# Two gated feed forward layers in split fp32: a low rank bank accumulated onto a negated copy, one VectorE sum less per group, and another queue order at the start

## The chip, the cores and the metric

The program runs on one core of a Trainium2 chip. The metric is device time in microseconds. Each execution is one launch of the whole computation. TensorE (PE) multiplies matrices, VectorE (DVE), ScalarE (ACT) and GpSimd (POOL) work on elements, SyncE (SP) only starts transfers. Each engine takes its own instructions in the order of the program, and engines wait for one another through semaphores.

## What is computed

1024 tokens of width 512 (8 blocks of 128) go through two gated feed forward layers, the first with a low rank addition chosen per block, the second behind an RMS norm, and the input is added at the end:

```python
def lora_add(base, inp, A, B):
    Ab = A[layer_idx][lora_indices]
    Bb = B[layer_idx][lora_indices]
    t = jnp.einsum('bri,bni->bnr', Ab, inp)
    return base + jnp.einsum('bor,bnr->bno', Bb, t) * SCALE
gate = lora_add(jnp.einsum('bnh,fh->bnf', x, W_gate), x, A_gate, B_gate)
up = lora_add(jnp.einsum('bnh,fh->bnf', x, W_up), x, A_up, B_up)
act = jax.nn.silu(gate) * up
down = lora_add(jnp.einsum('bnf,hf->bnh', act, W_down), act, A_down, B_down)
...
nx = x * jax.lax.rsqrt(var + RMS_EPS) * ln_w
g = jnp.einsum('bsh,ih->bsi', nx, gate_w)
u = jnp.einsum('bsh,ih->bsi', nx, up_w)
return jnp.einsum('bsi,hi->bsh', jax.nn.silu(g) * u, down_w)
...
x = x + _L0_ffn_ref(_L0_cond_ref(x, ...), ...)
```

The first layer has 1376 hidden features (ten tiles of 128 and a short one of 96), the second 1792 (14 tiles).

## The kernel before

**Precision.** Every fp32 operand is held as a high part (a rounding copy, made by ScalarE, names `hi_...`) and a low part (the difference, made by VectorE, names `lo_...`). A product of two 128x128 blocks with 512 tokens is three matmuls: high by high, high by low, low by high (`PASSES`).

**Fewer products.** The layers use a seven product scheme (Strassen's, in the form with shared sums) on 2x2 blocks: two feature tiles by two halves of the tokens (t = 0 and 1). A **group** j is one such 2x2 problem for gate or up; groups 0 to 7 (`S1` = 8) belong to the first layer, even j to gate and odd j to up. Its seven products on TensorE are `q1`, `g_prod`, `p6`, `q2`, `p3`, `p7`, and `p4`, each six matmuls. `p4(j-1)` is issued in group j, between `g_prod(j)` and `p6(j)`. In groups 0 to 7 `group_loras(j)` adds the low rank part between `p3` and `p7`: two matmuls of 256 columns each for `A_BANK`, `G_BANK` and `L_BANK` (which is `bank7`), and two more at the end of `p4`. The stacked low rank weights (`stack`) come in five chunks, copied by ScalarE (`stack_hi`) and completed by VectorE (`stack_lo`).

**Sums of products** go through copies between PSUM banks and the tile `mu`: ScalarE makes `ca(j)` (q1 into `B_BANK`), `cm(j)` (g into `mu`) and `cu(j)` (p6's bank into `mu`), and silus `c11`, `c12`, `c21`, `c22`; VectorE adds and multiplies (`c12`, `c22_sum`, `c22_act`, `c11`, `c21`). TensorE waits for `ca(j)` before `p6(j)`, for `cm(j)` before `p3(j)`, for `cu(j)` before `p7(j)` and for the first sum of `c22_sum(j-1)` (semaphore `s_b22`) before `p4(j-1)`. The second sum of `c22_sum(j)` subtracts the first from `L_BANK` and frees that bank for the next group's loras (`s_l22r`).

**Weights of group j + 1** are prepared during group j: `sums` (three sums on VectorE), `hi_a` and `hi_b` on ScalarE (blocks and sums), `lo_a` and `lo_b` on VectorE. The number in `lo_a(3)` is that of the load; load 2 belongs to group 0, load 3 to group 1. q1 needs the blocks (`lo_a`), `g_prod` the sums (`lo_b`).

**The start.** Before group 0 TensorE computes two feature tiles (units 0 to 3) and the short tile without the scheme. `short(t)` also projects the tokens on the low rank A; VectorE multiplies this by a mask (`t_mask`, out `traw`), ScalarE makes its high parts twice (`t_hi`, out `tgu`), VectorE its low part (`t_lo`), and then `first_loras(t)` can run. The scheme's four token sums are made by VectorE (`x_sum(0, i)`, out `xsum_c`), split by ScalarE (`hi_x`, out `xs`) and VectorE (`lo_t`); they are T1 to T4. T4 is first needed by `p4(0)`. ScalarE splits it in `last_block`. `short(1)` needs `unit_mul(0)` on VectorE before its second eighth.

**After group 7** the down projection begins with `main_c(0, 0)`. TensorE waits for the split down weights (`hi_wd`, `lo_wd`, out `wdc`), for the split activations (`hi_ac`, `lo_ac`, out `xs`), and for all `c11` of the first layer:

```python
pe.wait_ge(s_adlo, B)
pe.wait_ge(s_c11[0], S1 // 2)
pe.wait_ge(s_c11[1], S1 // 2)
...
    pe.wait_ge(s_alo, n + 1)
    pe.wait_ge(s_wdlo, n + 1)
```

VectorE's `group(7)` issues `lo_wd(0)` and `lo_ac(0)` ahead of `c11(7)` and `c12(7)`. All orders are written out by hand in the queue of each engine.

Of the kernel before, what the change touches and what calls it, by code (L numbers as in the profile page):

```python
# [22 lines left out]
S1, S2 = G1 - 2, G1 + NF - 4  # L23
# [20 lines left out]
def build(nc, xT_in, idx_in, wsh_in, w0_in, wgu_in, wd_in, vs_in, vj_in, agu_in, bgu_in, ad_in, bd_in, lnw_in, out):  # L44
# [4 lines left out]
    with ctx:  # L49
# [185 lines left out]
        s_s12, s_s22 = sem("c12_silu"), sem("c22_silu")  # L235
        s_c12, s_b22, s_l22r = sem("c12_summed"), sem("c22_summed"), sem("c22_with_lora")
        s_c12f, s_c22f = sem("c12_act"), sem("c22_act")
# [158 lines left out]
        def _(a):  # L396
# [37 lines left out]
            def cm(j):  # L434
                a.wait_ge(s_g, j + 1)
                if j >= 2 and j % 2 == 0:
                    a.wait_ge(s_b22, j - 1)
                elif j >= 2:
                    a.wait_ge(s_c22f, j // 2)
                copy(mu[:, j % 2, 0, :], G_BANK[j % 2][:, :]).then_inc(s_cm, 1)  # L440

# [24 lines left out]
            def c22(j):  # L466
                part = act_at(tiles_of(j)[1], 1)
                if j < S1:
                    a.wait_ge(s_l22r, j + 1)
                else:  # L470
                    a.wait_ge(s_b22, j + 1)
                silu(part, part, 1.0 if j < S1 else -1.0).then_inc(s_s22, 1)
# [208 lines left out]
            hi_a(2)  # L681
            a.wait_ge(s_xsum[0], 2)
            hi_x(0, T_SLOT[1], xsum_c[:, 1])
# [4 lines left out]
            t_hi(0)  # L688
            a.wait_ge(s_raw0_ld[1], 16 * 4)
            stack_rows(0, 1, slice(0, 32))  # L690
            unit_silu(0)
            unit_silu(1)
            short_silu(0)
            stack_rows(0, 1, slice(64, KS))
            stack_hi(1, 0)
# [133 lines left out]
        def _(v):  # L829
# [39 lines left out]
            def c22_sum(j):  # L869
                v.wait_ge(s_p7, j + 1)  # L870
                v.wait_ge(s_cm, j + 1)
                part, m5 = act_at(tiles_of(j)[1], 1), mu[:, j % 2, 0, :]
                to = part if j % 2 == 0 else m5
                nc.vector.tensor_tensor(to, m5, B_BANK[j % 2][:, :], ALU.add).then_inc(s_b22, 1)
                if j < S1:
                    v.wait_ge(s_b22, j + 1)
                    v.wait_ge(s_l22, j + 1)
                    nc.vector.tensor_tensor(to, L_BANK[:, :], to, ALU.subtract).then_inc(s_l22r, 1)

            def c22_act(j):  # L880
                part, m5 = act_at(tiles_of(j)[1], 1), mu[:, j % 2, 0, :]
                v.wait_ge(s_s22, j // 2 + 1)
                if j < S1:
                    v.wait_ge(s_l22r, j + 1)
                else:
                    v.wait_ge(s_b22, j + 1)
                nc.vector.scalar_tensor_tensor(part, m5, 1.0 if j < S1 else -1.0, part, ALU.mult, ALU.mult
# [426 lines left out]
        def _(pe):  # L1314
# [426 lines left out]
```

## Time and profile before

| what | value |
|---|---|
| median of three runs | 411.17 us (410.97 to 411.42) |
| profiled execution, its own time | 411.44 us |
| its span, first to last instruction | 409.4 us |
| TensorE busy | 401.3 us, 98% |
| VectorE busy | 319.7 us, 78% |
| ScalarE busy | 235.9 us, 58% |
| granted TensorE clock | 1.000 |

In the profile, PE is a matmul and PEld a weight load; busy matmul times are modelled to their ends, and neighbours overlap. A line such as L398 or L831 is that of a helper (`copy`, `sub`), so the tiles tell which step it is.

### The profile page before, as it was taken

What the parts mean: (1) busy time and instruction counts of PE and PEld (TensorE: products, weight loads), DVE (VectorE), ACT (ScalarE), POOL (GpSimd) and SP (SyncE); (2) the same over time, 40 slices, a digit from 0 to 9 for tenths busy, and PEclk for the clock granted to TensorE, in tenths of its full rate; (3) what the DMA queues carried; (4) which work ended last, traced back from release to release, by engine and by line L of the source; (5) the groups of instructions that cost most, each with busy time, mean ns of one, the idle gap of its engine ahead of it and who ended that gap; (6) DMA issues with size and microseconds to landing.
All of it is one profiled execution on the core that took longest, in us unless ns stands there. A gap on an engine that the chain in (4) does not pass through costs nothing.

```text
span 409.4 us, 5438 instructions
## 1 busy us (share of the span) xinstructions
PE 401.3 (98%) x1849; PEld 334.2 (82%) x1849; DVE 319.7 (78%) x491; ACT 235.9 (58%) x369; POOL 12.8 (3%) x16
## 2 busy tenths in 40 slices
PE   8989999999999999999999999999999999999996
PEld 6879788888888888888888888888888888888884
DVE  4699979696957567463889988779787869899992
ACT  4789785757563467631656555555655375384640
POOL 6300000000000100000000000000000000000000
PEclk9999999999999999999999999999999999999999
DMA  7630233311111420300101113132221125105112
GB/s 255 196 115 2 78 109 112 109 51 53 51 53 52 129 78 0 104 0 0 53 0 50 54 51 103 53 102 58 98 98 58 51 90 171 75 0 194 51 51 104
DMA packets 14237, 31.87 MB, mean 78 GB/s; under 512 B 2306, under 2 KB 4610, under 8 KB 14210
## 3 DMA queue, kind: packets, MB, share of 16 engines
q1 hardware_dynamic: 13632, 29.96, 23.2%
q10 hardware_dynamic: 578, 1.57, 1.1%
q8 instruction: 14, 0.23, 0.2%
q14 instruction: 13, 0.11, 0.1%
HBM read 29.43 MB, written 2.10 MB: 77 GB/s over the span
## 4 chain that ended last, share of the span: by engine, by line
PE 92%; DVE 4%; DMA 1%; issue 1%; ACT 1%; DVEq 0%; SPq 0%
PE bank L1320 45%; PE bank L1645 16%; PE bank L1510 15%; PE bank L1428 5%; PE bank L1456 3%; PE bank L1523 2%; PE bank L1330 2%; PE bank L1475 1%; PE bank L1464 1%; DMA wraw<-w_in 1%; DVE stack L831 1%; DVE xsum_c L1089 1%; ACT tgu L398 1%; PE bank L1530 0%; DVE act L916 0%
## 5 line engine op out<-in xcount | busy, mean ns | idle before, releaser
L1320 PE MATMUL bank<-xs,ws 128*128 128x512 f32 x840 | 194.2, 390 | 1.0 <-ACT mu L398 1.0
L1320 PEld LDWEIGHTS bank<-xs,ws 128*128 128x128 f32 x840 | 156.6, 188 | 33.2 <-ACT mu L398 1.4
L1510 PE MATMUL bank<-xs,wdc 128*128 128x512 f32 x264 | 62.9, 389 | 0.0
L1510 PEld LDWEIGHTS bank<-xs,wdc 128*128 128x128 f32 x264 | 49.3, 188 | 10.1
L398 ACT ACTIVATE xs<-act 128x512 fp32r<-128x512 f32 x71 | 43.0, 624 | 21.1 <-DVE act L981 7.5
L831 DVE TENSOR_TENSOR xs<-act,xs 128x512 fp32r<-128x512 f32 x71 | 47.6, 685 | 4.7 <-ACT xs L398 4.2
L831 DVE TENSOR_TENSOR ws<-wraw,ws 128x256 fp32r<-128x256 f32 (+2 forms) x49 | 32.4, 670 | 13.6 <-ACT ws L398 13.6
L398 ACT ACTIVATE bank<-bank 128x512 f32<-128x512 f32 x22 | 12.7, 580 | 45.7 <-PE bank L1320 45.7
L1645 PE MATMUL bank<-xs,vs 128*128 128x512 f32 x168 | 38.2, 389 | 0.0
L1645 PEld LDWEIGHTS bank<-xs,vs 128*128 128x128 f32 x168 | 31.5, 188 | 6.5
L398 ACT ACTIVATE ws<-wraw 128x256 fp32r<-128x256 f32 (+2 forms) x47 | 28.6, 620 | 11.7 <-PE bank L1320 4.1
L831 DVE TENSOR_TENSOR ws<-wsum,ws 128x1024 fp32r<-128x1024 f32 x20 | 24.5, 1226 | 12.7 <-ACT ws L398 12.7
L398 ACT ACTIVATE mu<-bank 128x512 f32<-128x512 f32 x40 | 23.9, 597 | 13.6 <-PE bank L1320 12.9
L1645 PE MATMUL bank<-xs,ws 128*128 128x512 f32 x126 | 29.0, 389 | 0.0
L1645 PEld LDWEIGHTS bank<-xs,ws 128*128 128x128 f32 x126 | 23.7, 188 | 4.9
L398 ACT ACTIVATE stack<-bgu_raw 32x1024 fp32r<-32x1024 f32 (+1 forms) x20 | 22.8, 1138 | 0.3
L1428 PE MATMUL bank<-xs,ws 128*128 128x512 f32 x96 | 22.1, 389 | 0.0
L451 ACT ACTIVATE act<-bank 128x512 f32<-128x512 f32 (+1 forms) x30 | 17.4, 593 | 7.6 <-PE bank L1330 6.2
L398 ACT ACTIVATE ws<-wsum 128x1024 fp32r<-128x1024 f32 x20 | 21.1, 1053 | 0.0
L1428 PEld LDWEIGHTS bank<-xs,ws 128*128 128x128 f32 x96 | 18.0, 188 | 3.7
L831 DVE TENSOR_TENSOR wdc<-wdr,wdc 128x512 fp32r<-128x512 f32 x11 | 7.6, 690 | 11.9 <-ACT wdc L398 11.8
L398 ACT ACTIVATE wdc<-wdr 128x512 fp32r<-128x512 f32 x11 | 6.9, 629 | 15.0 <-DMA wdr<-wd_in 15.0
(124 smaller groups left out, 446.1 us busy)
## 6 DMA issues: line engine op xcount, KB each, us to landing
wraw<-wgu_in SPq DMA_DIRECT2D x22, 512.0 KB, 3.4
wdr<-vs_in SPq DMA_DIRECT2D x7, 512.0 KB, 3.4
wdr<-wd_in SPq DMA_DIRECT2D x11, 256.0 KB, 2.7
wraw<-vj_in SPq DMA_DIRECT2D x3, 896.0 KB, 4.6
xa<-xT_in SPq DMA_DIRECT2D x4, 256.0 KB, 4.7
wraw<-w_in SPq DMA_DIRECT2D x4, 256.0 KB, 4.9
xa<-xT_in ACTq DMA_DIRECT2D x2, 512.0 KB, 6.4
bgu_raw<-bgu_in SPq DMA_DIRECT2D x32, 32.0 KB, 1.7
```

Source lines behind the costliest of these rows:

```text
L398: return nc.scalar.activation(out_ap, in_ap, ACT.Copy, scale=scale)
L451: return nc.scalar.activation(out_ap, in_ap, ACT.Silu, scale=scale)
L831: return nc.vector.tensor_tensor(out_ap, raw, v32(part), ALU.subtract)
L1089: nc.vector.scalar_tensor_tensor(s[:, i], s[:, min(i - 1, 1)], -1.0, half, ALU.mult, ALU.subtract).then_inc(s_xsum[ph], 1)
L1320: ins = mm(z[:, :], ws[:, j % 2, w, s, k * P:(k + 1) * P], xs[:, c, r, k, :], start=(start and k == 0 and s == 0 and r == 0), stop=(k == 1 ...
L1330: ins = mm(z[0:m, half], stk[c % 2][:, 2 * t + q, cols], t_op[:, half], start=(alone and q == 0), stop=(q == 1), skip_group_check=True)
L1428: ins = mm(z[:, :], ws[:, j % 2, w, s, (k % 2) * P:(k % 2) * P + P], x_op(k, t, r), start=(k == 0 and s == 0 and r == 0), stop=(k == KT - ...
L1456: mm(UNIT_BANK[i][g][:, :], w0_tile(s, k, g, i), x_op(k, 0, r), start=(k == 0 and s == 0 and r == 0), stop=(k == KT - 1 and r == 1), skip_ ...
L1464: mm(UNIT_BANK[n][g][:, :], w0_tile(s, k, g, UNITS[n][0]), x_op(k, 1, r), start=(k == 0 and s == 0 and r == 0), stop=(k == KT - 1 and s == ...
L1510: ins = mm(z[:, :], wd[:, s, h * P:(h + 1) * P], x[r], start=(start and s == 0 and r == 0), stop=False, skip_group_check=True)
L1523: ins = mm(T_BANK[t][:, :], ad[:, n, t, :], slot_c(u, r), start=(first and r == 0), stop=(last and r == 1), skip_group_check=True)
L1645: ins = mm(DOWN[p][3][h][:, :], down_w(i, s)[:, h * P:(h + 1) * P], slot_f(i, r), start=(p < 2 and k == 0 and s == 0 and r == 0), stop=(k ...
```

## The change

In groups 0 to 7 `cm(j)` now copies -G from its bank into `L_BANK`. The L loras accumulate onto it, a new ScalarE copy `cl(j)` takes the result to `mu` at the end of the group, and `c22_sum(j)` is one subtraction of `B_BANK`. TensorE no longer waits for `s_l22r` ahead of the L loras. At the start `t_mask(0)` and `t_hi(0)` come before the second token sum and its copy, the last four small low rank A splits come after `t_lo(0)` on VectorE, the second stack chunk's copies come after the silus, and `x_sum(0, 3)`, its copy and its low part come later.

```diff
             def cm(j):
                 a.wait_ge(s_g, j + 1)
+                if j == 0:
+                    a.wait_ge(s_um, 3)
+                elif j < S1:
+                    a.wait_ge(s_cl, j)
+                else:
+                    mu_free(j)
+                if j < S1:
+                    copy(L_BANK[:, :], G_BANK[j % 2][:, :], -1.0).then_inc(s_cm, 1)
+                else:
+                    copy(mu[:, j % 2, 0, :], G_BANK[j % 2][:, :]).then_inc(s_cm, 1)
...
+            def cl(j):
+                a.wait_ge(s_l22, j + 1)
+                mu_free(j)
+                copy(mu[:, j % 2, 0, :], L_BANK[:, :]).then_inc(s_cl, 1)
...
             def group(j, last):
                 ca(j)
-                if j == 0:
-                    last_block()
...
                 cu(j)
+                if j == 0:
+                    last_block()
                 if j + 1 < last:
                     hi_b(w_of(j + 1))
...
                 if j % 2 == 0:
                     c11(j)
+                if j < S1:
+                    cl(j)
...
-                nc.vector.tensor_tensor(to, m5, B_BANK[j % 2][:, :], ALU.add).then_inc(s_b22, 1)
                 if j < S1:
-                    v.wait_ge(s_b22, j + 1)
-                    v.wait_ge(s_l22, j + 1)
-                    nc.vector.tensor_tensor(to, L_BANK[:, :], to, ALU.subtract).then_inc(s_l22r, 1)
+                    v.wait_ge(s_cl, j + 1)
+                    nc.vector.tensor_tensor(to, m5, B_BANK[j % 2][:, :], ALU.subtract).then_inc(s_b22, 1)
...
             stack_lo(0, 0)
-            x_sum(0, 1)
             v.wait_ge(s_maskr, 1)
             t_mask(0)
+            x_sum(0, 1)
+            lo_t(0, 0)
+            t_lo(0)
             for b in range(4, B):
                 lo_agu(b)
-            lo_t(0, 0)
-            t_lo(0)
...
                     lo_a(w_of(j + 1))
+                    if j == 0:
+                        x_sum(0, 3)
                     lo_b(w_of(j + 1))
+                if j == 0:
+                    lo_t(0, 3)
...
-                if j >= 1:
-                    pe.wait_ge(s_l22r, j)
-                else:
+                if j == 0:
                     pe.wait_ge(s_tneg, 1)
-                    pe.wait_ge(s_um, 3)
-                group_lora(L_BANK, j, 1, 1, alone=True).then_inc(s_l22, 1)
+                group_lora(L_BANK, j, 1, 1).then_inc(s_l22, 1)
```

VectorE's queue at the first mask, before (the row of `traw` is `t_mask(0)`, that of `tgu` is `t_lo(0)`, `short_w_lo` are the small splits):

```order
L1089 SCALAR_TENSOR_TENSOR xsum_c<-xsum_c,xa1 128x1024 [waits x_sum_c]
L922 TENSOR_TENSOR traw<-bank0,mask 32x512 [waits short_projected,mask_repeated]
L922 TENSOR_TENSOR traw<-bank5,mask 32x512
L831 TENSOR_TENSOR short_w_lo<-agu_raw,xs 128x2x4x16 [waits agu_hi] x4
L831 TENSOR_TENSOR xs<-xsum_c,xs 128x1024 [waits x_hi_c]
L831 TENSOR_TENSOR tgu<-traw,tgu 32x1024 [waits t_masked,t_hi]
```

and now:

```order
L934 TENSOR_TENSOR traw<-bank0,mask 32x512 [waits short_projected,mask_repeated]
L934 TENSOR_TENSOR traw<-bank5,mask 32x512
L1101 SCALAR_TENSOR_TENSOR xsum_c<-xsum_c,xa1 128x1024 [waits x_sum_c]
L846 TENSOR_TENSOR xs<-xsum_c,xs 128x1024 [waits x_hi_c]
L846 TENSOR_TENSOR tgu<-traw,tgu 32x1024 [waits t_masked,t_hi]
L846 TENSOR_TENSOR short_w_lo<-agu_raw,xs 128x2x4x16 [waits agu_hi] x4
```

The token sum moved behind the mask products, and the small splits behind `t_lo(0)`.

ScalarE's queue in group 0, before (`ca(0)`, `last_block`, `cm(0)`, `hi_a(3)`, `cu(0)`, `hi_b(3)`, `c11(0)`):

```order
L398 ACTIVATE bank2<-bank0 128x512 [waits unit_silu,q1_done]
L398 ACTIVATE xs<-xsum_c 128x1024 [waits unit_up,x_sum_c]
L398 ACTIVATE mu<-bank5 128x512 [waits g_done]
L398 ACTIVATE ws<-wraw 128x3x256 [waits unit_up,w_loaded_odd]
L398 ACTIVATE mu<-bank2 128x512 [waits p6_done]
L398 ACTIVATE ws<-wsum 128x4x256 [waits w_sums,unit_up,w_loaded_odd]
```

and now, up to `cl(0)`:

```order
L398 ACTIVATE bank2<-bank0 128x512 [waits unit_silu,q1_done]
L398 ACTIVATE bank7<-bank5 128x512 [waits unit_act,g_done]
L398 ACTIVATE ws<-wraw 128x3x256 [waits unit_up,w_loaded_odd]
L398 ACTIVATE mu<-bank2 128x512 [waits p6_done]
L398 ACTIVATE xs<-xsum_c 128x1024 [waits unit_up,x_sum_c]
L398 ACTIVATE ws<-wsum 128x4x256 [waits w_sums,unit_up,w_loaded_odd]
L467 ACTIVATE act<-bank0 128x512 [waits q2_done]
L398 ACTIVATE mu<-bank7 128x512 [waits l22_done]
```

The copy of the token sum moved from ahead of `cm(0)` to between `cu(0)` and `hi_b(3)`, and the copy out of `bank7` is new.

ScalarE's queue at the end of group 7, before (`c21(6)`, `cu(7)`, then `hi_wd(0)`, `hi_ac(0)`, `hi_wd(1)`):

```order
L451 ACTIVATE act<-bank2 128x512 [waits p4_done]
L398 ACTIVATE mu<-bank4 128x512 [waits c12_act,p6_done]
L398 ACTIVATE wdc<-wdr 128x512 [waits stack_lo,wd_loaded_even]
L398 ACTIVATE xs<-act 128x512 [waits g_done,unit_act]
L398 ACTIVATE wdc<-wdr 128x512 [waits wd_loaded_odd]
```

and now:

```order
L467 ACTIVATE act<-bank2 128x512 [waits p4_done]
L398 ACTIVATE mu<-bank4 128x512 [waits c12_act,p6_done]
L398 ACTIVATE mu<-bank7 128x512 [waits c22_act,l22_done]
L398 ACTIVATE wdc<-wdr 128x512 [waits stack_lo,wd_loaded_even]
L398 ACTIVATE xs<-act 128x512 [waits g_done,unit_act]
L398 ACTIVATE wdc<-wdr 128x512 [waits wd_loaded_odd]
```

Here `cl(7)`, with its wait for the L loras, came in ahead of `hi_wd(0)`.

## Rows read from the trace of the kernel before

**Rows 1.** The page, busy us, share of the span and instructions of each engine

```profile
PE 401.3 (98%) x1849; PEld 334.2 (82%) x1849; DVE 319.7 (78%) x491; ACT 235.9 (58%) x369; POOL 12.8 (3%) x16
```

**Rows 2.** Busy time by stretch: from:to, its length, busy by engine, PEclk, DMA share, GB/s

```profile
27.00:52.00 25.00, 22.70 (x133) 19.63 (x133) 23.90 (x28) 20.62 (x25) 0.00 (x0) 1.00 0.12 35
30.83:47.60 16.77, 16.77 (x106) 15.16 (x105) 16.36 (x19) 14.05 (x16) 0.00 (x0) 1.00 0.17 48
50.45:405.70 355.25, 355.19 (x1600) 294.73 (x1600) 278.68 (x432) 199.55 (x321) 2.79 (x4) 1.00 0.22 70
```

**Rows 3.** Instructions in time order, the first mask: start, us, engine, line, operation, [idle before]

```profile
23.14 1.22 DVE L1089 SCALAR_TENSOR_TENSOR xsum_c<-xsum_c,xa 128x1024 f32<-128x1024 f32 x1
...
24.40 1.30 DVE L922 TENSOR_TENSOR traw<-bank,mask 32x512 f32<-32x512 f32 x2
...
25.36 0.89 ACT L398 ACTIVATE xs<-agu_raw 128x128 fp32r<-128x128 f32 x4
...
25.73 0.90 DVE L831 TENSOR_TENSOR short_w_lo<-agu_raw,xs 128x128 fp32r<-128x128 f32 x4
26.16 2.13 ACT L398 ACTIVATE tgu<-traw 32x1024 fp32r<-32x1024 f32 x2
26.55 1.22 DVE L831 TENSOR_TENSOR xs<-xsum_c,xs 128x1024 fp32r<-128x1024 f32 x1
...
27.51 0.84 PE L1464 MATMUL bank<-xs,first_w 128*128 128x512 f32 x3
...
28.32 1.22 DVE L831 TENSOR_TENSOR tgu<-traw,tgu 32x1024 fp32r<-32x1024 f32 x1 [0.56 <-ACT tgu L398]
...
29.64 1.67 PE L1330 MATMUL bank<-tgu,stack 128*128 128x256 f32 x12 [1.29 <-issue]
...
30.83 1.28 DVE L916 TENSOR_TENSOR act<-act,bank 128x512 f32<-128x512 f32 x2
...
31.15 0.64 PE L1475 MATMUL bank<-xs 128*128 128x256 f32 x4
```

**Rows 4.** Instructions in order of time, groups 0 and 1

```profile
42.38 1.59 PE L1330 MATMUL bank<-tgu,stack 128*128 128x256 f32 x12
...
43.81 5.63 PE L1320 MATMUL bank<-xs,ws 128*128 128x512 f32 x24
...
47.60 1.22 DVE L1089 SCALAR_TENSOR_TENSOR xsum_c<-xsum_c,xa 128x1024 f32<-128x1024 f32 x1
...
48.86 1.06 ACT L398 ACTIVATE xs<-xsum_c 128x1024 fp32r<-128x1024 f32 x1 [2.88 <-DVE xsum_c L1089]
...
50.45 1.65 PE L1320 MATMUL bank<-xs,ws 128*128 128x512 f32 x6 [1.01 <-ACT mu L398]
...
52.61 1.23 DVE L831 TENSOR_TENSOR ws<-wsum,ws 128x1024 fp32r<-128x1024 f32 x1 [0.26 <-ACT ws L398]
52.66 5.63 PE L1320 MATMUL bank<-xs,ws 128*128 128x512 f32 x24
...
54.35 0.68 DVE L874 TENSOR_TENSOR act<-mu,bank 128x512 f32<-128x512 f32 x1
...
58.12 0.40 PE L1330 MATMUL bank<-tneg,stack 128*128 128x256 f32 x2
```

**Rows 5.** Instructions in order of time, the end of group 7

```profile
123.06 0.60 ACT L398 ACTIVATE mu<-bank 128x512 f32<-128x512 f32 x1 [0.79 <-PE bank L1320]
123.56 0.62 ACT L398 ACTIVATE wdc<-wdr 128x512 fp32r<-128x512 f32 x1
...
125.58 0.88 PE L1330 MATMUL bank<-tgu,stack 128*128 128x256 f32 x6
126.02 0.69 DVE L894 TENSOR_TENSOR act<-act,bank 128x512 f32<-128x512 f32 x1 [0.51 <-PE bank L1330]
...
127.68 2.88 PE L1510 MATMUL bank<-xs,wdc 128*128 128x512 f32 x12
```

**Rows 6.** Instructions in order of time, TensorE's warm-up

```profile
1.14 3.86 PE L1439 MATMUL bank<-ones 128*128 128x512 f32 x9 [1.14 <-DVE eps L1097]
```

More of the change, by code:

```diff
@@ L235, in build @@
         s_s12, s_s22 = sem("c12_silu"), sem("c22_silu")
-        s_c12, s_b22, s_l22r = sem("c12_summed"), sem("c22_summed"), sem("c22_with_lora")
+        s_c12, s_b22, s_cl = sem("c12_summed"), sem("c22_summed"), sem("l22_copied")
         s_c12f, s_c22f = sem("c12_act"), sem("c22_act")
@@ L435, in cm, with mu_free @@
                 a.wait_ge(s_g, j + 1)
+                if j == 0:
[8 more added lines that the diff above has]
+                    copy(mu[:, j % 2, 0, :], G_BANK[j % 2][:, :]).then_inc(s_cm, 1)
+            def mu_free(j):
                 if j >= 2 and j % 2 == 0:
@@ L439, in cm @@
                     a.wait_ge(s_c22f, j // 2)
-                copy(mu[:, j % 2, 0, :], G_BANK[j % 2][:, :]).then_inc(s_cm, 1)
+            def cl(j):
+                a.wait_ge(s_l22, j + 1)
+                mu_free(j)
+                copy(mu[:, j % 2, 0, :], L_BANK[:, :]).then_inc(s_cl, 1)
             def cu(j):
@@ L467, in c22 @@
                 part = act_at(tiles_of(j)[1], 1)
-                if j < S1:
-                    a.wait_ge(s_l22r, j + 1)
-                else:
-                    a.wait_ge(s_b22, j + 1)
+                a.wait_ge(s_b22, j + 1)
                 silu(part, part, 1.0 if j < S1 else -1.0).then_inc(s_s22, 1)
@@ L681, in _ @@
             hi_a(2)
-            a.wait_ge(s_xsum[0], 2)
-            hi_x(0, T_SLOT[1], xsum_c[:, 1])
+            t_hi(0)
             a.wait_ge(s_short, 1)
@@ L687, in _ @@
                 hi_agu(b)
-            t_hi(0)
-            a.wait_ge(s_raw0_ld[1], 16 * 4)
-            stack_rows(0, 1, slice(0, 32))
+            a.wait_ge(s_xsum[0], 2)
+            hi_x(0, T_SLOT[1], xsum_c[:, 1])
             unit_silu(0)
@@ L693, in _ @@
             short_silu(0)
+            a.wait_ge(s_raw0_ld[1], 16 * 4)
+            stack_rows(0, 1, slice(0, 32))
             stack_rows(0, 1, slice(64, KS))
@@ L870, in c22_sum @@
                 v.wait_ge(s_p7, j + 1)
-                v.wait_ge(s_cm, j + 1)
                 part, m5 = act_at(tiles_of(j)[1], 1), mu[:, j % 2, 0, :]
                 to = part if j % 2 == 0 else m5
-                nc.vector.tensor_tensor(to, m5, B_BANK[j % 2][:, :], ALU.add).then_inc(s_b22, 1)
                 if j < S1:
-                    v.wait_ge(s_b22, j + 1)
-                    v.wait_ge(s_l22, j + 1)
-                    nc.vector.tensor_tensor(to, L_BANK[:, :], to, ALU.subtract).then_inc(s_l22r, 1)
+                    v.wait_ge(s_cl, j + 1)
+                    nc.vector.tensor_tensor(to, m5, B_BANK[j % 2][:, :], ALU.subtract).then_inc(s_b22, 1)
+                else:
+                    v.wait_ge(s_cm, j + 1)
+                    nc.vector.tensor_tensor(to, m5, B_BANK[j % 2][:, :], ALU.add).then_inc(s_b22, 1)
             def c22_act(j):
@@ L882, in c22_act @@
                 v.wait_ge(s_s22, j // 2 + 1)
[L883 to L886, printed above, removed]
+                v.wait_ge(s_b22, j + 1)
                 nc.vector.scalar_tensor_tensor(part, m5, 1.0 if j < S1 else -1.0, part, ALU.mult, ALU.mult
@@ L1152, in _ @@
             stack_lo(1, 1)
-            x_sum(0, 3)
             def group(j, first, last):
@@ L1163, in group @@
                     sums(w_of(j + 1))
-                if j == 0:
-                    lo_t(0, 3)
                 if j > S1 and j % 2 == 0:
@@ L1393, in group_loras @@
                 group_lora(G_BANK[j % 2], j, 0, 1).then_inc(s_p3, 1)
-                if j >= 1:
-                    pe.wait_ge(s_l22r, j)
-                else:
+                if j == 0:
                     pe.wait_ge(s_tneg, 1)
-                    pe.wait_ge(s_um, 3)
-                group_lora(L_BANK, j, 1, 1, alone=True).then_inc(s_l22, 1)
+                group_lora(L_BANK, j, 1, 1).then_inc(s_l22, 1)
             def p7(j):
@@ L1550, in _ @@
                     p4(S1 - 1)
-                    pe.wait_ge(s_l22r, S1)
+                    pe.wait_ge(s_b22, S1)
                     t_c(0, 0, True, False).then_inc(s_use, 1)
```

## The prediction, made before the changed kernel ran

> **What bounds the kernel now.** I read the busy shares first, then busy time by stretch, then the rows in order of time around the places the change touches. TensorE is busy 98% of the span and VectorE 78% [rows 1], so an operation taken from VectorE is worth something only where TensorE waits for VectorE. From 50.45 to 405.70 us TensorE is busy 355.19 of 355.25 us; between 27 and 52 us it is busy 22.70 of 25 [rows 2]. So the group loop has no pause that could be won. There are two pauses worth looking at, both before it.
>
> Pause A: the first low rank products start at 29.64 after 1.29 us idle, and 0.10 before that VectorE ended its `tgu` low part, 28.32 + 1.22 = 29.54 [rows 3]. Undisturbed they would start at 27.51 + 0.84 - 0.16 = 28.19, since in an unbroken stream a group starts 0.16 before the modelled end of the one ahead (42.38 + 1.59 against 43.81 [rows 4]). A costs 1.45.
>
> Pause B: p3(0) starts at 50.45 after 1.01 idle and waited for ScalarE's `mu` copy, which stood behind the copy of the fourth token sum, started at 48.86 when VectorE ended that sum (47.60 + 1.22) [rows 4]. Undisturbed it would start at 43.81 + 5.63 - 0.16 = 49.28. B costs 1.17. Together 2.62 us can be won at most.
>
> **Mask first (A).** VectorE is free at 23.14, where the second token sum starts [rows 3]. Now the two mask products (1.30) come first and end at 24.44, and ScalarE makes both high parts from 24.48 to 26.61 (2.13 [rows 3]). VectorE: sum 24.47 to 25.69, low part of T1 25.61 to 26.83 (neighbours on all 128 rows overlap by 0.08, as 25.73 + 0.90 against 26.55), then the `tgu` low part 26.86 to 28.08. With the release of 0.10 that is 28.18 against 28.19: A is gone.
> Behind it stands what was put off. Four small low parts (0.90) run 28.11 to 29.01, the low part of T2 (1.22) 28.93 to 30.15; its high part is ready near 28.5 (26.61, the four small copies of 0.89, one copy of 1.06). So unit_mul(0) runs 30.07 to 30.75 (0.76 earlier than now, 30.83 [rows 3]), and TensorE sees it about 30.83. It needs it at the second 0.72 us piece of short(1): before, 31.15 + 0.72 = 31.87, a margin; now 28.19 + 1.51 + 0.72 = 30.42. (0.72 is (42.38 - 31.15 - 5.46) / 8, with 5.46 for 24 matmuls from 52.66 to 58.12 [rows 3, 4].) A new pause of 0.4; TensorE is 1.04 ahead after it, 1.0 with the slower first step after a pause (p3(0), below).
>
> **Fourth sum later (B).** ScalarE's copy of g(0) no longer stands behind it, and TensorE at p3(0) doesn't wait. But the sum now stands ahead of two other things that group 1 needs. On VectorE it comes after the three weight sums and lo_a(3), and ScalarE waits for it in `last_block` ahead of hi_b(3); lo_b(3) then waits for hi_b(3). VectorE did not stop between 30.83 and 47.60 (16.36 busy of 16.77 [rows 2], the rest is hand-over), so it enters this part 0.75 early. The same work that now ends where lo_b(3) starts, 52.61, less its idle 0.26 and less the low part of T4 (1.14 with overlap), then ends at 52.61 - 0.26 - 1.14 - 0.75 = 50.46 [rows 4]. From there: copy 1.06 and hi_b, another 1.06 on as many elements, 0.1 overlapped, to 52.5; lo_b(3), 1.23, ends at 53.8. TensorE needs it for g(1) at 52.66 + 2 x 1.365 - 1.0 - 1.3 = 53.1: a pause of 0.75. Then low part of T4, c12(0) and c22_sum(0) follow. That last one ends at 54.35 + 0.68 now [rows 4]; less 0.75, less 0.26, and with the new idle time of 2.1 it ends at 56.1. TensorE needs it for p4(0), which starts now at 58.12 - 1.365 = 56.76, and would start at 56.2. The first product after a pause takes 0.13 longer: p3(0) took 1.49 to the next start, not 1.365 (52.66 less 0.72 for the loras less 50.45 [rows 4]). **Gain left when p4(0) has run: 56.76 - 56.2 - 0.13 = 0.4 us of the 2.6.** The bounds: 0 if VectorE's chain slips by 0.4, 2.6 if ScalarE's wait is hidden. I take 0.4: both ends of that chain are read from rows of the same form.
>
> **Low rank bank on the negated copy.** VectorE loses eight sums of about 0.7 (as the row at 54.35 [rows 4]); TensorE's instructions are the same, and it loses its wait for VectorE ahead of the L products. ScalarE gains eight copies out of `bank7`, 0.60 each (the `mu` copy at 123.06 [rows 5]); the copy of G goes to the bank in place of `mu` at the same size. In groups 0 to 6 the new copy starts 0.92 after the first lora (six steps of 0.12, from twelve in 43.81 - 42.38 [rows 4], then 0.2 for the last to end and release) and falls in time in which ScalarE is free. Two stack copies of the size of the copy at 48.86 (1.06 [rows 4]) follow it, to 0.92 + 0.5 + 2.1 = 3.5 after the loras start. q1 of the next group, whose copy is ScalarE's next work, ends at 0.72 + 1.365 x 2 + 0.2 = 3.65, and TensorE needs that copy only for p6, some 3 us on. Covered, price zero; the end of the saved sums too, since TensorE doesn't wait there.
>
> **Group 7 is where it isn't covered.** There the next thing in ScalarE's queue is the first high part of the down weights. It now starts at 123.56, straight behind cu(7), and its like for the activations follows; c11(7) on VectorE waits only for the loras and starts at 126.02. TensorE takes main_c(0, 0) at 127.68 without a pause [rows 5]. In the new queue cl(7) stands ahead of both copies and waits for the last lora of group 7: 125.58 + 0.92 = 126.50. Then `wdc` high part 127.00 to 127.63, activation high part to 128.14; VectorE's `wdc` low part 127.66 to 128.34, activation low part 128.26 to 128.95, and c11(7), behind them in VectorE's queue, 128.87 to 129.56. main_c(0, 0) waits for both low parts and for c11(7): it starts at 129.63, not 127.68. With 0.13 for the first step that is **a new pause of 2.1 us**, in the time of the kernel before. Bounds: 1.4 if TensorE needed only the two low parts, 2.2 with 0.1 more of release. I take 2.1, the queue order fixes it. What follows (c22_sum(7), p4(7), the next weights, whose load waits for the low parts) moves with it, and TensorE runs unbroken to the end, so nothing is given back.
>
> **Sum.** -0.4 + 2.1 = +1.7 us. The profiled execution took 411.44 (span 409.4), 0.27 over the median 411.17. I forecast 413.1 for a profiled run and 411.17 + 1.65 = 412.8 for the median, 0.4% slower.
>
> **Rivals.**
> 1. Full recovery at the start, the pause in group 7 stays: -2.6 + 2.1 gives 410.6 to 410.7, no change that can be told. For it: A and B each have one named waiter. Against it: the margins above of -0.4 and -0.75 us.
> 2. Faster: the copies of group 7 are done before TensorE needs them, and 0.4 to 2.6 remains, 408.6 to 410.8. From the start of cl(7) to TensorE's release are 3.13 us, so it decides if that copy starts before 127.68 - 3.13 = 124.55. The last lora starts at 126.2 [rows 5], which speaks against it.
> 3. The new copy delays each group: it pushes the small `ad` copies of group 6 by 0.5, and by my count TensorE's p4(6) keeps 0.3. If such margins fail in two or three groups by 0.3, the time is 413.5 to 414.
> 4. The clock falls in the new pause. The granted clock stays 1.00 through pauses of 1.29 and 1.01 [rows 2, 3, 4], but this one is 1.95. The nine warm-up matmuls at 1.14 took 3.86, so 0.43 each [rows 6] against 0.228 later (5.46 / 24): half speed for 3.86 us costs 1.9 more, 414.7. The Trainium skill (TensorE: Matmul & The Clock Gate, HAM oscillation) says that idle gaps between bursts of matmuls send the engine back to 1.2 GHz; by that rule this case, by the two rows at full clock after a pause my forecast. No run here shows a pause this long.
>
> **How the numbers follow.** A measurement of this kernel can tell about 0.2%, 0.8 us, from no change. Forecast 0.73, rival 1 0.12, rival 2 0.06, rival 3 0.05, rival 4 0.04. The range takes the forecast with start gains of 0 to 1.2 and an end price of 1.9 to 2.2 (411.7 to 413.5) and reaches down to rival 1: 410.6 to 413.6. The forecast itself falls within 0.2% in some 3 of 73. Faster 0.07, same 0.15, slower 0.78.
>
> **What would show it.** Right: no idle before the first loras and before p3(0); small pauses at the second piece of short(1), g(1) and p4(0); one of about 2 us before the first `wdc` matmul, with ScalarE's copy out of `bank7` straight ahead of its first `wdc` copy. Wrong: TensorE unbroken there, or more than 1.5 us won before group 2, or idle time inside groups 2 to 7.

## The result and the profile after

The changed kernel takes 413.26 us (median of 13 executions, 412.58 to 415.99), the kernel before 411.68 in the same session (13, 410.97 to 412.39). The ratio is 1.0051 [1.0034, 1.0069]: slower, as forecast. The median lies 0.46 over my 412.8 and within the range. The ratio goes by means, and the mean says more: 413.82 us, above my upper end of 413.6, where the kernel before has a mean of 411.70. In the profile TensorE's end moved by what the sum said, to 0.02 us; the rest came from things that the sum did not hold: the clock falling in some executions, a late start of TensorE in others, and a kernel before that is slower on average than the profile and the three times I had.

The page of the changed kernel, busy us, share of the span and instructions, beside [rows 1]:

```profile
PE 402.3 (98%) x1849; PEld 334.3 (81%) x1849; DVE 314.2 (77%) x483; ACT 240.0 (58%) x377; POOL 12.7 (3%) x16
```

VectorE lost 5.5 us of work in eight instructions and ScalarE gained 4.1 in eight, and the span is 410.7 in place of 409.4. Busy time by stretch, columns as in [rows 2]:

```profile
27.00:57.00 30.00, 28.56 (x160) 24.41 (x159) 27.36 (x35) 25.54 (x33) 0.00 (x0) 1.00 0.15 48
57.78:127.10 69.32, 69.32 (x332) 58.05 (x330) 45.21 (x68) 45.54 (x71) 0.00 (x0) 1.00 0.23 69
127.10:129.17 2.07, 0.17 (x2) 0.03 (x1) 2.07 (x4) 1.49 (x3) 0.00 (x0) 1.00 0.26 41
129.17:407.30 278.13, 278.10 (x1232) 229.81 (x1232) 220.00 (x347) 149.39 (x245) 2.79 (x4) 1.00 0.22 69
```

TensorE idles 1.44 us between 27 and 57, not at all from p6(1) at 57.78 to the end of group 7, some 1.9 before the down projection, and hardly (0.03) after it. Instructions of the changed kernel in time order at the first mask, beside [rows 3]:

```profile
24.27 2.15 ACT L398 ACTIVATE tgu<-traw 32x1024 fp32r<-32x1024 f32 x2 [0.47 <-DVE traw L934]
...
26.66 1.22 DVE L846 TENSOR_TENSOR tgu<-traw,tgu 32x1024 fp32r<-32x1024 f32 x1
...
28.13 1.60 PE L1343 MATMUL bank<-tgu,stack 128*128 128x256 f32 x12
...
29.98 1.28 DVE L928 TENSOR_TENSOR act<-act,bank 128x512 f32<-128x512 f32 x2
...
30.72 0.74 PE L1485 MATMUL bank<-xs 128*128 128x256 f32 x4 [0.27 <-DVE act L928]
```

The first loras start at 28.13 without idle time (forecast 28.19, before 29.64), and the second piece of short(1) waits 0.27 for the unit that `lo_t(0, 1)` now precedes. The same view at groups 0 and 1, beside [rows 4]:

```profile
49.14 1.22 DVE L1101 SCALAR_TENSOR_TENSOR xsum_c<-xsum_c,xa 128x1024 f32<-128x1024 f32 x1
...
50.40 1.06 ACT L398 ACTIVATE xs<-xsum_c 128x1024 fp32r<-128x1024 f32 x1 [2.73 <-DVE xsum_c L1101]
51.36 1.04 ACT L398 ACTIVATE ws<-wsum 128x1024 fp32r<-128x1024 f32 x1
...
52.44 1.23 DVE L846 TENSOR_TENSOR ws<-wsum,ws 128x1024 fp32r<-128x1024 f32 x1 [2.08 <-ACT ws L398]
...
53.72 1.66 PE L1333 MATMUL bank<-xs,ws 128*128 128x512 f32 x6 [0.50 <-DVE ws L846]
...
55.31 0.68 DVE L890 TENSOR_TENSOR act<-mu,bank 128x512 f32<-128x512 f32 x1
...
56.05 1.65 PE L1333 MATMUL bank<-xs,ws 128*128 128x512 f32 x6 [0.67 <-DVE act L890]
```

ScalarE's copy of the token sum (50.40) stands ahead of its copy of `wsum` (51.36), VectorE waits 2.08 us for that, and TensorE waits for VectorE twice: 0.50 before g(1), 0.67 before p4(0). p4(0) starts at 56.05 (forecast 56.2, before 56.76). The end of group 7, beside [rows 5]:

```profile
125.01 0.88 PE L1343 MATMUL bank<-tgu,stack 128*128 128x256 f32 x6
...
125.92 0.60 ACT L398 ACTIVATE mu<-bank 128x512 f32<-128x512 f32 x1 [2.84 <-PE bank L1343]
126.41 0.62 ACT L398 ACTIVATE wdc<-wdr 128x512 fp32r<-128x512 f32 x1
...
127.07 0.69 DVE L846 TENSOR_TENSOR wdc<-wdr,wdc 128x512 fp32r<-128x512 f32 x1 [8.09 <-ACT wdc L398]
...
128.28 0.68 DVE L906 TENSOR_TENSOR act<-act,bank 128x512 f32<-128x512 f32 x1
...
129.17 3.01 PE L1520 MATMUL bank<-xs,wdc 128*128 128x512 f32 x12 [1.90 <-DVE act L906]
```

`cl(7)` waits 2.84 us for the loras with the first `wdc` copy behind it; VectorE has stood still for 8.09 when that copy ends; c11(7) is the last releaser. The last piece of the chain that ended last is one row in each kernel, here of the changed one and then of the one before:

```profile
343.37 63.93 PE bank L1655 x282
```

```profile
341.74 63.93 PE bank L1645 x282
```

TensorE ends at 407.30 in place of 405.67: **+1.63, forecast +1.65**. Part of that match is luck: the start gave 0.58 in place of 0.4, and the end of group 7 took 0.58 + 1.63 = 2.21 in place of 2.1.

### The profile page after: what moved, and what is told of

The parts are those of the page before. It is cut to its first block, busy times and chain, and to the rows that moved or that the text cites. A ratio compares the mean times of both kernels' runs of the same rounds, so it can differ in the third digit from the quotient of the medians.

```text
span 410.7 us, 5437 instructions
## 1 busy us (share of the span) xinstructions
PE 402.3 (98%) x1849; PEld 334.3 (81%) x1849; DVE 314.2 (77%) x483; ACT 240.0 (58%) x377; POOL 12.7 (3%) x16
## 4 chain that ended last, share of the span: by engine, by line
PE 90%; DVE 5%; ACT 1%; issue 1%; DMA 1%; DVEq 0%; SPq 0%; ACTq 0%
PE bank L1333 44%; PE bank L1655 16%; PE bank L1520 15%; PE bank L1438 5%; PE bank L1466 3%; PE bank L1533 2%; PE bank L1343 2%; PE bank L1485 1%; PE bank L1474 1%; DMA wraw<-w_in 1%; DVE stack L846 1%; DVE xs L846 1%; DVE xsum_c L1101 1%; DVE act L928 1%; ACT tgu L398 1%
## 5 line engine op out<-in xcount | busy, mean ns | idle before, releaser
L398 ACT ACTIVATE bank<-bank 128x512 f32<-128x512 f32 x30 | 17.4, 580 | 39.6 <-PE bank L1333 38.7
L846 DVE TENSOR_TENSOR stack<-bgu_raw,stack 32x1024 fp32r<-32x1024 f32 (+1 forms) x10 | 13.2, 1322 | 2.9 <-ACT stack L398 2.7
```

The costliest lines, as they stand in the source:

```text
L398: return nc.scalar.activation(out_ap, in_ap, ACT.Copy, scale=scale)
L846: return nc.vector.tensor_tensor(out_ap, raw, v32(part), ALU.subtract)
```

## Experiments

### Which part does what

**e1_cl7_later** takes only the new copy of group 7 out of the way:

```diff
-                if j < S1:
+                if j < S1 - 1:
                     cl(j)
...
                 hi_wd(n)
                 hi_ac(n)
+                if n == 0:
+                    cl(S1 - 1)
```

> The changed kernel with one edit: in group 7 the ScalarE copy out of bank7 is issued behind the first copies of the down weights and of the activations, not ahead of them. Theory (queue order costs 2.1 us there): the pause before main_c(0, 0) is gone, the profiled span falls from 410.7 to about 408.7, the median lies about 0.4 us under the kernel before, and no run lies 1.3 us or more above the others, since the pause in which the clock could fall is gone. Rival (the pause is set by something else, such as the last lora sum itself): the pause stays, span 410.7.

Median 410.82, ratio 0.9969 [0.9952, 0.9985] (12 executions): this order is faster than both kernels, 0.3% under the kernel before. Its rows at the end of group 7:

```profile
124.15 0.62 ACT L398 ACTIVATE xs<-act 128x512 fp32r<-128x512 f32 x1
...
126.36 1.55 PE L1335 MATMUL bank<-xs,ws 128*128 128x512 f32 x6
126.56 0.60 ACT L398 ACTIVATE mu<-bank 128x512 f32<-128x512 f32 x1 [1.79 <-PE bank L1345]
...
127.75 2.88 PE L1522 MATMUL bank<-xs,wdc 128*128 128x512 f32 x12
```

The copy runs in idle time of ScalarE and TensorE goes on: 1.39 us from p7(7) to main_c(0,0), against 129.17 - 125.72 = 3.45 in the changed kernel. That the queue position of one copy costs 2.06 is shown. TensorE ends at 405.74, 1.56 before the changed kernel's, though p7(7) started 0.64 later there (126.36 against 125.72). But that is still 0.07 behind TensorE's end in the kernel before, and the time is some 1.3 us shorter. So these two profiles do not show where e1's lead over the kernel before comes from. Part of it may be the shorter tail, taken up below; it was not isolated.

**e2_bank_only** has the change of the bank with the start order of the kernel before; **e3_start_only** has the new start order in the kernel before. The core of e2's edit against the changed kernel (e3's against the kernel before is its reverse):

```diff
             stack_lo(0, 0)
+            x_sum(0, 1)
             v.wait_ge(s_maskr, 1)
             t_mask(0)
-            x_sum(0, 1)
...
                 ca(j)
+                if j == 0:
+                    last_block()
```

> The low rank bank part alone, with the order at the start as in the kernel before. Theory (its parts add): pauses A and B as before, none in groups 1 to 6, the pause of 2.0 us before main_c(0, 0): span 409.4 + 2.1 = 411.5, time 2.1 us over the kernel before, or 3.5 to 3.8 where the clock falls too. Rival (the missing VectorE sum gives something back in the groups): under 1.5 us over.

> The order at the start alone, the low rank bank as in the kernel before. Theory: 0.5 us under the kernel before (span 408.9 to 409.0), since pauses A and B (2.6 us) are replaced by pauses at the second piece of short(1), at g(1) and at p4(0). Rival (the small pauses come from the new bank copies in group 0): 2 us or more under the kernel before.

e2: median 413.67, ratio 1.0047 [1.0023, 1.0071] (6 executions), with pauses A (1.53 in front of 29.76), B (1.02 in front of 50.57) and the one of group 7 (1.90 in front of 129.86). e3: median 412.06, ratio 0.9997 [0.9984, 1.001] (10). In e3 TensorE ends at 405.28, 0.39 before the kernel before (forecast 0.4), and yet its span is 410.3. e3, with the old bank, has the same three small pauses as the changed kernel (0.35, 0.51 and 0.68), so they come from the new start order and not from the new copies in group 0. The bank carries the loss, and the start gains on TensorE what I summed. In the time this gain can't be told: 0.4 us is 0.1%, and e3's interval holds it as well as no change. That the span did not follow TensorE's end needed runs of its own, below.

**e5_both** puts `cl(7)` as in e1 and also `last_block` behind `hi_b(3)`; **e6_all_three** also takes unit_mul(0) ahead of lo_t(0, 1):

```diff
                 cu(j)
+                if j + 1 < last:
+                    hi_b(w_of(j + 1))
                 if j == 0:
                     last_block()
                 if j + 1 < last:
-                    hi_b(w_of(j + 1))
...
```

```diff
+            unit_mul(0)
             lo_t(0, 1)
-            unit_mul(0)
```

> The changed kernel with two edits: cl(7) behind the first weight and activation copies, and in group 0 ScalarE's copy of the fourth token sum behind hi_b(3). Theory (lo_b(3) and c22_sum(0) were late by ScalarE's wait for that sum): no pause at g(1) and p4(0), so 1.7 us less than with the first edit alone; TensorE ends 2.2 us before it does in the kernel before. Rival (VectorE's work itself is late there): under 1 us less than with the first edit alone.

> The two edits before and a third: VectorE issues unit_mul(0) ahead of the low part of the second token sum. Theory: the pause in short(1) goes too, another 0.3 to 0.4 us, so that TensorE ends 2.6 us before it does in the kernel before. Rival (something else is late right behind it): no more than the two edits give.

e5: median 409.35, ratio 0.9929 [0.991, 0.9948] (6), **the best version here**. Its rows at groups 0 and 1, and its busy time from 31 to 400 us:

```profile
48.63 1.06 ACT L398 ACTIVATE ws<-wsum 128x1024 fp32r<-128x1024 f32 x1 [0.81 <-DVE wsum L863]
49.30 1.22 DVE L1104 SCALAR_TENSOR_TENSOR xsum_c<-xsum_c,xa 128x1024 f32<-128x1024 f32 x1
...
50.44 1.22 DVE L849 TENSOR_TENSOR ws<-wsum,ws 128x1024 fp32r<-128x1024 f32 x1
50.45 5.63 PE L1336 MATMUL bank<-xs,ws 128*128 128x512 f32 x24
50.55 1.06 ACT L398 ACTIVATE xs<-xsum_c 128x1024 fp32r<-128x1024 f32 x1 [0.86 <-DVE xsum_c L1104]
```

```profile
31.00:400.00 369.00, 368.99 (x1688) 307.58 (x1689) 290.78 (x444) 218.94 (x346) 2.79 (x4) 1.00 0.22 69
```

With `wsum` copied first, VectorE's low part follows at once and both pauses of group 1 are gone. TensorE ends at 403.46, 2.21 before it does in the kernel before, as expected. This is nearly the full recovery at the start that rival 1 described (0.27 at the second piece of short(1) stays), had from the same parts by order alone. e6: median 409.27, ratio 0.9931 [0.991, 0.9952] (6), no gain over e5. The pause in short(1) is gone, but one of 0.51 in front of the low rank products of the second half of the tokens, which e5 does not have, came in its place:

```profile
41.40 1.69 PE L1346 MATMUL bank<-tgu,stack 128*128 128x256 f32 x12 [0.51 <-DVE tgu L849]
```

### Why some executions take longer

Seven of 33 executions of the changed kernel (three sessions) report a mean granted clock of 0.996, and nine others, at clock 1.000, take 1.4 us or more over the mean of the 17 that are left (412.94), the undisturbed ones below. **after_again** and **after_third** are the changed kernel without an edit.

> The changed kernel once more, beside the others. Theory (about 1.6 us slower in what TensorE does, and a few executions longer by the landing of the last stores): most executions 1.5 to 1.7 us over the kernel before on this chip, mean 1.6 to 2.0 over. Rival (the change itself makes long executions frequent): again about half of them 1.3 us or more above the lowest group.

> The changed kernel for the third time, to count its long executions beside those of the next kernel. Theory (two causes of long executions: full speed comes late at the start, in any kernel, and the clock falls in the pause of 2 us): some executions with a mean clock of 0.996, about one in four, 1.7 us over the others. Rival (one cause only, the start): no more at 0.996 than in the kernel with the pause filled.

Ratios 1.0054 [1.0032, 1.0076] (8 executions) and 1.0032 [1.0013, 1.0051] (12). **e4_filler**, and the same on another chip as **e4_again**, issue eight matmuls on ones into a free bank, with results thrown away, in the pause of group 7:

```diff
             pe.wait_ge(s_c11[0], S1 // 2)
+            for i in range(8):
+                mm(bank[0][:, :].rearrange("p (k n) -> p k n", k=KT), ones[:, :], ...)
             pe.wait_ge(s_c11[1], S1 // 2)
```

> The changed kernel with eight matmuls of 512 columns on the tile of ones ahead of the waits of main_c(0, 0), 1.8 us of TensorE work that is thrown away and lies in the pause. Theory (executions that are 1.3 us or more over the others are those in which the clock falls after this pause): the fast executions keep their time, about 1.6 us over the kernel before, and the long ones vanish, so that all runs lie within 0.8 us. Rival (the long executions come from the start of the program, where the kernel before has a spread too): four or so of ten stay 1.3 us over the rest.

> The changed kernel with the pause filled by eight thrown-away matmuls, for the second time, on the chip of the run before it. Theory: no execution at 0.996, a few that are 2 us longer at 1.00, and a mean 0.4 us or more below that of the changed kernel. Rival: the same share of long executions and the same mean.

Ratios 1.0014 [1.0, 1.0029] and 1.0022 [1.0005, 1.0039], 12 executions each. **e7_pause_doubled** and **e8_pause_one_more** lengthen the pause: the copy out of `bank7` in group 7 is made four times and twice. **e9_doubled_filled** is e7 with 16 such matmuls in the pause.

```diff
+                if j == S1 - 1:
+                    for i in range(3):
+                        copy(mu[:, j % 2, 0, :], L_BANK[:, :]).then_inc(s_more, 1)
+                        a.wait_ge(s_more, i + 1)
                 copy(mu[:, j % 2, 0, :], L_BANK[:, :]).then_inc(s_cl, 1)
```

> The changed kernel with ScalarE's copy out of bank7 in group 7 made four times, each after the one ahead. Theory (each us ahead of the weight copies is a us of pause, and the clock stays): the pause grows from 2.0 to 4.0 us, the time by 2.0 us, granted clock 1.00 behind the pause. Rival (the clock falls in a pause that is long enough): matmul steps behind the pause of 0.43 us in place of 0.228, granted clock 0.5 for a stretch, the time 3 us or more over the changed kernel.

> The changed kernel with the copy out of bank7 in group 7 made twice, so that the pause is 2.6 us. Theory (the clock falls in part of the executions, the more so the longer the pause): 0.6 us over the changed kernel where the clock stays, 2.4 us over it where it falls, and more than one execution in four of that kind. Rival (it falls only with the pause of 3.8 us): 0.6 us over the changed kernel, no execution at 0.996.

> The changed kernel with the copy out of bank7 made four times, and sixteen thrown-away matmuls of 512 columns ahead of the waits of main_c(0, 0), so that the pause of 3.8 us is mostly filled. Theory (the clock falls by TensorE's idle time): granted clock 1.00 behind it, steps of 0.228 us, the time 2.0 us over the changed kernel and 2 us or so under the one with the pause unfilled. Rival (it falls by something else in that kernel): steps of 0.43 us again.

e7: ratio 1.0124 [1.0093, 1.0155] (4 executions). e8: 1.0083 [1.0052, 1.0114] (4). e9: 1.0062 [1.0043, 1.0082] (9). The first matmuls behind the pause in e7, e8 and e9, one fence each:

```profile
131.16 5.46 PE L1524 MATMUL bank<-xs,wdc 128*128 128x512 f32 x12 [3.79 <-DVE act L910]
```

```profile
131.90 4.57 PE L1524 MATMUL bank<-xs,wdc 128*128 128x512 f32 x12 [2.53 <-DVE act L910]
```

```profile
127.01 3.79 PE L1558 MATMUL bank<-ones 128*128 128x512 f32 x16
130.81 3.01 PE L1524 MATMUL bank<-xs,wdc 128*128 128x512 f32 x12
```

The same 12 matmuls took 3.01 in the changed kernel behind a pause of 1.90. In the stretches of e7 the column before the DMA share is the granted clock:

```profile
128.00:131.00 3.00, 0.00 (x0) 0.00 (x0) 1.93 (x4) 2.59 (x5) 0.00 (x0) 0.89 0.01 3
131.00:132.00 1.00, 0.83 (x2) 0.77 (x3) 0.96 (x2) 0.00 (x0) 0.00 (x0) 0.50 0.65 250
...
135.00:138.00 3.00, 3.00 (x10) 2.33 (x10) 0.00 (x0) 0.00 (x0) 0.00 (x0) 0.64 0.27 87
138.00:200.00 62.00, 62.00 (x280) 51.44 (x279) 34.98 (x58) 31.93 (x54) 2.79 (x4) 1.00 0.18 51
```

In e7 the clock falls to 0.50, that is 1.2 GHz, within the pause of 3.79 us and comes back between 135 and 138 us. In e8 it falls later:

```profile
129.00:131.00 2.00, 0.37 (x2) 0.00 (x0) 1.20 (x2) 2.00 (x5) 0.00 (x0) 1.00 0.01 4
131.00:133.00 2.00, 1.10 (x5) 0.96 (x6) 1.97 (x5) 0.32 (x1) 0.00 (x0) 0.98 0.51 131
133.00:135.00 2.00, 2.00 (x7) 1.52 (x6) 1.90 (x5) 1.15 (x2) 0.00 (x0) 0.50 0.00 0
135.00:137.00 2.00, 2.00 (x7) 1.58 (x6) 0.61 (x2) 0.00 (x0) 0.00 (x0) 0.66 0.48 127
```

The clock is still up when main_c(0,0) starts at 131.90 and falls about 1 us into it, while TensorE is busy: the fall belongs to the pause but need not lie in it. From main_c(0,0) to the next main_c TensorE took 6.51 us in e8 (131.90 to 138.41), 7.69 in e7 (131.16 to 138.85) and 4.90 in the changed kernel (129.17 to 134.07). So the price of a fall was 1.6 us in e8 and 2.8 in e7, whose clock was low for longer. Seven executions of the changed kernel have e8's mean clock, 0.996 (the profiled one of e7 has 0.992), and four of the seven have spans of 412.3 to 412.8 against a mean of 410.9 for the undisturbed ones, which fits e8's price; the other three are longer still. All executions by their mean clock:

| kernel | idle at group 7 | at 0.992 to 0.996 |
|---|---|---|
| kernel before (later sessions) | none | 1 of 107 |
| changed | 1.9 | 7 of 33 |
| e2 | 1.9 | 2 of 6 |
| changed, padded (e11, below) | 1.9 | 1 of 7 |
| e8 | 2.5 | 4 of 4 |
| e7 | 3.8 | 4 of 4 |
| e4, filled | 0 | 0 of 24 |
| e9, e7 filled | 0 | 0 of 9 |
| e1, e5, e6 | none | 0 of 24 |
| before_again, e3, e10 | none | 0 of 34 |

The pause makes the clock fall in part of the executions, and filling it takes these away: that is shown. The one execution of the kernel before at 0.996 stays without an explanation. No profile of the changed kernel caught such an execution; that the fall in them is the one seen in e7 and e8 is read from the mean clock.

The nine long ones at clock 1.000 are another matter, since filling does not take them away (6 of 24 in e4). The profile of after_again is one of them. PE matmuls (first bracket) in two early stretches, first in the changed kernel's profile, then in after_again's:

```profile
6.00:8.00 2.00, 2.00 (x9) 1.65 (x10) 1.70 (x4) 1.16 (x3) 2.00 (x2) 1.00 1.00 355
8.00:10.00 2.00, 2.00 (x10) 1.64 (x10) 1.95 (x4) 1.15 (x2) 2.00 (x2) 1.00 1.02 373
```

```profile
6.00:8.00 2.00, 2.00 (x5) 1.61 (x6) 1.49 (x4) 0.94 (x2) 2.00 (x2) 1.00 1.00 363
8.00:10.00 2.00, 2.00 (x6) 1.52 (x6) 2.00 (x4) 1.36 (x3) 2.00 (x2) 1.00 1.05 394
```

Half the matmuls until 10 us, though the granted clock reads 1.00 in both. `short` starts at 18.94 in place of 16.91, and TensorE ends at 409.28 in place of 407.30: nothing between gives the 2.0 back. Two more late profiles with the new start order agree: e4_again has `short` 1.67 later than e4_filler (18.74 against 17.07) and TensorE's end 1.46 later, e11 (below) 1.70 and 1.75 later than the changed kernel. **before_again** is the kernel before once more:

> The kernel before, unchanged, for a second profile. Open: its executions have a median 0.8 us above its profiled one, while those of the changed kernel don't, so the clock time moves less than TensorE's. Theory (in the kernel before, an instruction load that falls beside the last store delays its landing): two q14 instruction packets in the last 9 us and a landing of the last ScalarE store of 2.5 to 3.8 us, against 2.1 us and none in the changed kernel. Rival: a landing of 2.1 us in this execution, and the difference elsewhere.

Ratio 1.0003 [0.9991, 1.0016] (12). Its profile also has the late start (5 and 6 matmuls in these stretches), and yet TensorE ends only 0.3 later than in the first profile:

```profile
29.36 0.84 PE L1464 MATMUL bank<-xs,first_w 128*128 128x512 f32 x3
30.04 1.24 PE L1330 MATMUL bank<-tgu,stack 128*128 128x256 f32 x9
```

The loras follow at 30.04 without idle time: 1.85 behind the 28.19 of an unbroken stream, but 0.40 behind the 29.64 of [rows 3]. The work of VectorE and ScalarE that pause A waited for is done by then, so the pause takes 1.45 of the delay: it was slack for a TensorE that starts late. The mask first removed pause A, and with it this cover. That is one late profile with pause A against three without it. In the times, the kernel before has no execution among 107 above 413.46 (median 412.19), and the changed kernel has nine among 33, at clock 1.000, from 414.37 up. With the old start order e2 and e10 have none that is long at full clock either; with the new one e1 has 2 of 12, e4 6 of 24 and e9 2 of 9. But e3, e5 and e6 have the new start order too, and of their 22 executions none is 1.2 us over its kernel's median. The cover does not explain that, so it is shown in profiles, and its share in the times is only likely.

### The end behind TensorE

From TensorE's end to the end of the span are 3.4 to 3.5 us in every profile of a kernel with the new bank (13 of 13), but 3.7 and 4.5 in the two of the kernel before, 5.0 in e3 and 4.8 in e10. DMA queues and issues in the last microseconds of before_again, then of the changed kernel:

```profile
q14 instruction: 2, 0.02, 2.1%
...
out<-act ACTq DMA_DIRECT2D x1, 128.0 KB, 3.2
```

```profile
q1 hardware_dynamic: 288, 0.39, 21.1%
q10 hardware_dynamic: 144, 0.13, 7.5%
...
out<-act ACTq DMA_DIRECT2D x1, 128.0 KB, 2.1
```

In the kernels with the old bank the last store of ScalarE's queue takes 2.5 to 3.8 us to land, and instruction packets of queue q14 stand between 407 and 409 us in all four; in the others it takes 2.1 and no q14 packet stands behind TensorE's end. Two runs asked what decides it. **e10_before_padded** adds eight one-column copies on ScalarE to the kernel before (377 instructions, as changed); **e11_vector_padded** adds eight on VectorE to the changed one (491, as before):

```diff
+                copy(stat[:, 1:2], stat[:, 0:1]).then_inc(s_idle, 1)
```

```diff
+                nc.vector.tensor_copy(stat[:, 1:2], stat[:, 0:1]).then_inc(s_idle, 1)
```

> The kernel before with eight more ScalarE instructions, one at the end of each of groups 0 to 7: a copy of one column, which nothing reads. ScalarE then has as many instructions as in the changed kernel. Theory (where the instruction load falls depends on the number of instructions): no q14 packet in the last 9 us, the last store lands in 2.1 us, TensorE ends where it does in the kernel before (within 0.3 us), and the mean lies 0.5 to 1 us under that of the kernel before. Rival (the landing varies by itself): the same mean as the kernel before.

> The changed kernel with eight tiny VectorE copies of one column, one behind each of groups 0 to 7, so that VectorE has 491 instructions, as the kernel before had, in place of 483. Theory (how many instructions VectorE has decides where its instruction fetches fall, and with eight more one falls into the last microseconds): TensorE ends within 0.3 us of the changed kernel's 407.30, instruction packets lie in the last 3 us, the last ScalarE store takes 2.5 to 3.8 us to land in place of 2.1, and the time is 0.5 to 1 us over the changed kernel's, mean 414.3 to 414.8 on a quiet chip (ratio 1.0055 to 1.007). Rival (the number of VectorE instructions has nothing to do with it): no instruction packets in the last 3 us, the store lands in 2.1 us, ratio 1.003 to 1.0055 as for the changed kernel.

e10: ratio 0.9998 [0.9987, 1.0009] (12), landing 3.5, one such packet: not the number of ScalarE's instructions. e11: ratio 1.006 [1.0033, 1.0086] (7), landing 2.1, no such packet there, and TensorE's end at 409.05 comes with 5 and 7 matmuls in the two early stretches. So VectorE's number isn't it either, and its higher ratio likely has the causes of the section above. What sets the place of these packets stays open; that the tail is longer where they stand is seen in four of four profiles, but no run moved them while leaving the rest as it was, so they may only go with the long tail and not cause it.

## Why the prediction was right or wrong

- **Pauses A and B, and the three that follow them:** right. A and B are gone, and the three new ones stand where they were put, with 0.27, 0.50 and 0.67 us idle (forecast 0.4, then 0.75 and the wait for p4(0)). The gain left at p4(0) was put at 0.4; from p6(1), 58.36 before, 57.78 now, it was 0.58.
- **New copy free in groups 0 to 6:** right, 69.32 of 69.32 us busy. Rival 3 falls.
- **Group 7, +2.1:** right in size (pause 1.90, and 3.45 from p7 to main_c against 1.39 in e1: 2.06), in place and in releaser. Rivals 1 and 2 fall: the copy started at 125.92, after 124.55.
- **Sum on TensorE:** +1.63 against +1.65, both terms 0.1 to 0.2 larger than forecast and opposite in sign.
- **Step that failed: the clock behind the new pause, which the sum put at nothing** ("by the two rows at full clock after a pause my forecast", rival 4 at 0.04). I took the clock as one thing or the other and gave the fall a small chance, since pauses up to 1.29 had kept the clock. It is a share of executions: 7 of 33 at 1.9 us idle. In the first 13, by which the forecast is measured, three fell, with a mean of 415.03 against 412.95 for the seven undisturbed. They add 3/13 x 2.08 = 0.48 to the mean; without it the mean would be 413.34, within the range. The Trainium skill (TensorE: Matmul & The Clock Gate, HAM oscillation) gives its rule for idle gaps longer than this pause, so it did not ask for a fall here, and rival 4 took it further than the Trainium skill does. The profiles of the changed kernel agree with the rule as it is given (clock 1.00 from 127.10 on), but 7 of its 33 executions do not, nor do all four of e8. The price was nearly right, 1.9 against 1.6 in e8 (2.8 in e7). The term should have been a share times a price in the sum, and the range should have held it.
- **A term that was not there: the cover that a removed pause gave.** Pause A was priced at 1.45 to be won. In the one late profile of the kernel before it also takes 1.45 of 1.85 us of the delay, and the end comes 0.3 later in place of 2.0. Three late ones among the first 13 (mean 414.61) add 3/13 x 1.66 = 0.38; that they are late starts is read from their times.
- **The base.** The forecast of 412.8 stands on the median of three, 411.17. In the 13 executions beside the changed kernel's first 13 the mean is 411.70, and in all later ones 412.16. The profiled one, with a tail of 3.7, was shorter than most. This base is 0.53 of the 1.0 us by which the mean of 413.82 lies above the forecast; the other 0.47 is a difference of 2.12 in place of 1.65: +1.26 for the undisturbed ones, 0.48 for the falls, 0.38 for the late ones.

The parts of the difference over all sessions, from 33 executions of the changed kernel (mean 413.86) and 107 of the one before (412.16): the 17 undisturbed ones of the changed kernel have a mean of 412.94, that is +0.78. The nine late ones (mean 414.76) add 9/33 x 1.82 = 0.50, the seven at 0.996 (mean 414.93) add 7/33 x 1.99 = 0.42. Together 1.70, 0.41%. Of TensorE's +1.63 some 0.85 is not seen in the undisturbed ones; the tail, shorter by 0.3 to 1.6 in the profiles, is of the size to account for it, but that share was not isolated.

So the forecast difference of 1.65 came close to these 1.70 for a reason that was not its own, by luck: something behind TensorE, perhaps the shorter tail, took about what late starts and clock falls gave.

## What to carry to other kernels

An operation that a change adds on an engine with time to spare may cost nothing in the steady loop, as here in groups 0 to 6, and its whole wait where the loop ends: look at what its queue holds next at each border, and put the work that TensorE waits for ahead of it (here one line moved was 2.06 us). A pause of TensorE can have a price beside its length: behind 1.9 us the clock fell here in 10 of 46 executions. And an old pause that is removed may have been the slack for a late start. So a sum over one profiled execution wants a share of such executions with it, and the time of before from many.

## What the runs showed of the hardware

- At 1.9 us idle the clock fell in 10 of 46 executions (changed, e2, e11), at 2.5 and 3.8 in 8 of 8. In e8 the fall came about 1 us after TensorE had started again. The half speed cost 1.6 us in e8 and 2.8 in e7. At 1.0 to 1.5 (pauses A and B in the kernel before and in e2) no profile shows a fall.
- TensorE may run at half rate until 10 us, with matmuls from 1.14 on, in 5 of 17 profiles, while the granted clock reads 1.00. What decides it stays open.
- Instruction packets of q14 between TensorE's end and the span's go with a last store of 2.5 to 3.8 us in place of 2.1, in 4 of 17 profiles. The clock also falls after the last matmul in some executions, at no cost, as in this stretch of e3. Half speed for 2.3 of 410.3 us lowers the mean to 0.997, the value of that execution, so means of 0.997 to 0.999 may well come from there.

```profile
408.00:410.30 2.30, 0.00 (x0) 0.00 (x0) 0.00 (x0) 0.00 (x0) 0.00 (x0) 0.50 0.00 0
```
